# Two bursts of value products per head, half-ready one-hots and earlier first keys in a sparse-attention and soft-mixture block

## What is computed

```python
scores = jnp.einsum('bhqd,bhkd->bhqk', q, k) * scale
sparsity = scores.max(axis=-1) - scores.mean(axis=-1)
_, top_idx = jax.lax.top_k(sparsity, U)                 # U = 307
q_sel = jnp.take_along_axis(q, top_idx[..., None], axis=2)
scores_sel = jnp.einsum('bhud,bhkd->bhuk', q_sel, k) * scale
attn = jax.nn.softmax(scores_sel, axis=-1)
out_sel = jnp.einsum('bhuk,bhkd->bhud', attn, v)
out = jnp.zeros_like(q).at[bi, hi, top_idx].set(out_sel)
```

## Time and profile before

| what | us |
|---|---|
| median of 3 runs | 1648.62 (1648.59 to 1650.77) |
| the profiled execution, its own time | 1640.96 |
| its span in the trace | 1638.9 |
| attention of batch 0, first gather to last turn | 455.3 to about 596 |
| attention of batch 1 | 952.8 to about 1091 |

### The profile page before, as it was taken

One profiled execution on the slowest core, in us unless ns is written; L12 is line 12 of the kernel. 1 busy time (PEld: TensorE's weight loads), 2 busy tenths in 40 slices (PEclk: granted clock), 3 DMA queues, 4 the chain that ended last, 5 costly groups with the idle time before them and its releaser, 6 DMA issues.

```text
span 1638.9 us, 28513 instructions
## 1 busy us (share of the span) xinstructions
PE 1501.4 (92%) x8674; PEld 837.0 (51%) x8674; DVE 1218.9 (74%) x2910; ACT 1041.9 (64%) x1404; POOL 267.0 (16%) x317
## 2 busy tenths in 40 slices
PE   7989999998779999999998989989999999989999
PEld 3532222223345532222222745544788986479988
DVE  6689999999866759999999887856756443675511
ACT  4588888887546678888887547763343473333464
POOL 2430000004413362000000213341111000111100
PEclk9999999999989999999999999999999999999999
DMA  5751111131522201111112211120134302014410
GB/s 187 245 154 39 51 45 39 39 97 39 165 63 68 64 19 39 50 47 39 39 40 89 67 32 50 53 64 24 39 123 162 102 29 77 0 33 156 163 48 32
DMA packets 93457, 119.38 MB, mean 73 GB/s; under 512 B 22862, under 2 KB 78766, under 8 KB 92860
## 3 DMA queue, kind: packets, MB, share of 16 engines
q1 hardware_dynamic: 90300, 117.66, 23.5%
q0 software_dynamic: 3072, 0.66, 0.4%
HBM read 93.46 MB, written 24.79 MB: 72 GB/s over the span
## 4 chain that ended last, share of the span: by engine, by line
PE 46%; DVE 33%; issue 13%; DMA 3%; ACT 3%; POOL 1%; SPq 0%; DVEq 0%; ACTq 0%; POOLq 0%
DVE work_area L1239 25%; PE psum L2045 7%; PE psum L2109 6%; PE psum L1890 5%; PE psum L1913 5%; PE psum L1988 4%; PE psum L1904 4%; PE psum L2056 3%; DVE big_area L1239 2%; PE psum L2065 2%; DMA work_area<-heads_out 2%; PE psum L2099 2%; PE psum L1746 1%; PE psum L1721 1%; ACT big_area L919 1%
## 5 line engine op out<-in xcount | busy, mean ns | idle before, releaser
L1239 DVE CUSTOM_DVE_ANT_0 work_area<-psum,work_area 128x1024 f32<-128x1024 f32 x512 | 589.3, 1220 | 9.5 <-PE psum L1782 5.5
L849 ACT ACTIVATE work_area<-psum 128x1024 f32<-128x1024 f32 x512 | 510.4, 1026 | 78.1 <-DVE big_area L1239 29.1
L1782 PE MATMUL psum<-work_area 96*128 96x512 bf16 x1024 | 310.7, 385 | 48.1 <-DVE big_area L1239 7.5
L1772 PE MATMUL psum<-work_area 96*128 96x512 bf16 x1024 | 306.0, 381 | 7.7 <-ACT work_area L849 2.3
L1782 PEld LDWEIGHTS psum<-work_area 96*128 96x128 bf16 x1024 | 63.8, 97 | 266.9 <-DVE big_area L1239 250.8
L867 ACT ACTIVATE work_area<-psum 128x614 f32<-128x614 f32 x192 | 124.0, 681 | 87.7 <-PE psum L1904 87.5
L1772 PEld LDWEIGHTS psum<-work_area 96*128 96x128 bf16 x1024 | 89.1, 98 | 153.3 <-ACT work_area L849 58.6
L703 POOL DMA_INDIRECT heads_out<-work_area x96 | 98.0, 1021 | 190.9 <-DVE work_area L1394 169.8
L1988 PE MATMUL psum<-slots_T,work_area 128*128 128x512 f32 x256 | 117.5, 603 | 0.0
L2045 PE MATMUL psum<-work_area,xn 128*128 128x128 f32 x1024 | 117.2, 275 | 0.0
L2109 PE MATMUL psum<-expert_out,work_area 128*128 128x256 f32 x512 | 115.6, 379 | 1.1 <-ACT work_area L984 1.1
(11 more groups left out here) (255 smaller groups left out, 2046.4 us busy)
## 6 DMA issues: line engine op xcount, KB each, us to landing
work_area<-in_L_ffn_w_dram SPq DMA_DIRECT2D x32, 1024.0 KB, 5.5
work_area<-k_parts SPq DMA_DIRECT2D x192, 64.2 KB, 2.1
work_area<-q_parts SPq DMA_DIRECT2D x192, 64.0 KB, 2.2
k_parts<-work_area SPq DMA_DIRECT2D x24, 384.0 KB, 4.0
q_parts<-work_area SPq DMA_DIRECT2D x16, 384.0 KB, 2.5
big_area<-q_parts SPq DMA_DIRECT2D x16, 384.0 KB, 5.3
work_area<-k_parts SPq DMA_DIRECT2D x32, 192.0 KB
x_res<-in_L_attn_x_dram SPq DMA_DIRECT2D x8, 512.0 KB, 6.7
```

The costliest lines, as they stand in the source:

```text
L849: s.activation(SC[:, t % 4], PS[:, 2 * (n % 2):2 * (n % 2) + 2].rearrange("p a n -> p (a n)"), ACT.Relu).then_inc(relu_done, 1)
L1239: v.tensor_tensor_reduce(SC[:, t % 4], PS[:, 4 + 2 * (t % 2):6 + 2 * (t % 2)].rearrange("p a n -> p (a n)"), SC[:, t % 4], 1.0, -3.0e38, A ...
L1772: last = mm(PS[:, 2 * (n % 2) + k], QS1[par][0:TERMS, t * P:(t + 1) * P], KS[par][0:TERMS, k * 512:(k + 1) * 512], start=True, stop=True)
L1782: last = mm(PS[:, 4 + 2 * (t % 2) + k], QS1[par][0:TERMS, t * P:(t + 1) * P], KS[par][0:TERMS, K1 + k * 512:K1 + (k + 1) * 512], start=Tru ...
```

## The change

Four things are changed, all in the attention or just ahead of it.

1. The value products of a head come in two bursts of eight key tiles in place of four bursts of four, and there are eight `PX` buffers in place of four. The new buffers overlap the parts' area, so in the first head of batch 0 ACT waits for the last parts (`parts_ready`) before the seventh exponential, and SP issues the next batch's terms only when the head's gather is done (`gathered`, h + 3).
2. The one-hot gives a signal at its half (`oh_half_ready`), and the gathers are cut into halves of eight: the second half for the next head stands after this head's steps 2 and 3, the first half for the head after next behind steps 6 and 7, ahead of `turn` and of the signal `k2_used`.
3. `take_queries` moves from ahead of the eighth exponential to behind the fourth (in the first head behind the sixth); `rows` moves from the third burst to ahead of steps 4 and 5.
4. SP fetches the first two heads' keys of batch 0 and the ones ahead of all stores of batch 1's parts; before, the ones stood behind the store of unit 8 and the keys behind that of unit 12. (The ones are the constant rows under the keys.)

```diff
@@ memory
+        PX_last = [a.take([2, UP]) for _ in range(2)]
...
+        a = Area(zeros, 2 * UP)
+        PX += [a.take([2, UP]) for _ in range(2)] + PX_last
@@ SP, attention_keys, and the order of the queue
                         if h < 14:
+                            sp.wait_ge(gathered, h + 3)
                             key_term(1, (h - 2) // 6 * DH, (h - 2) // 6, k)
...
+            key_ones(0)
+            for par in range(2):
+                first_keys(0, par)
             for u in range(NU):
                 parts_to_dram(1, u)
                 if u == share(G + 1)[-1]:
                     queries_to_sbuf(0, 3)
-                if u == 8:
-                    key_ones(0)
-                if u == 12:
-                    for par in range(2):
-                        first_keys(0, par)
@@ ACT
-                        act.wait_ge(p_used, b * 64 + i * 8 + (par * 4 + k // 2 + 1))
-                        slot = k % 4
-                        s.activation(PX[slot][:, :, 0:U], PS[:, 2 * (k % 2):2 * (k % 2) + 2, 0:U], ACT.Exp, scale=SCALE).then_inc(p_ready, 1)
+                        act.wait_ge(p_used, b * 32 + i * 4 + par * 2 + k // 4 + 1)
+                        s.activation(PX[k][:, :, 0:U], PS[:, 2 * (k % 2):2 * (k % 2) + 2, 0:U], ACT.Exp, scale=SCALE).then_inc(p_ready, 1)
...
-                    for k in range(7):
+                    first = i == 0 and par == 0
+                    for k in range(8):
+                        if b == 0 and first and k == 6:
+                            act.wait_ge(parts_ready, B * NU)
                         exps(i, par, (k,))
-                        if b == 0 and i == 0 and par == 0 and 1 <= k <= 3:
+                        if b == 0 and first and 1 <= k <= 3:
                             second_part(1, NU - 4 + k)
-                    if more:
-                        take_queries(i, 1 - par, par + 1)
-                    exps(i, par, range(7, 8))
++                        if more and k == (5 if first else 3):
+                            take_queries(i, 1 - par, par + 1)
@@ DVE, onehot
+                        if not pieces and t == NT // 2 - 1:
+                            last.then_inc(oh_half_ready, 1)
@@ PE
-                            pe.wait_ge(oh_ready, b * H + i * 2 + (n + 1))
+                            pe.wait_ge(oh_half_ready, b * (H - 1) + i * 2 + n)
...
+                        elif t == NT // 2:
+                            pe.wait_ge(oh_ready, b * H + i * 2 + (n + 1))
...
-                def pe_head(i, n, first, later):
-                    CUTS = (0, 0, NT // 2, NT) if first else (0, 5, 11, NT)
-                    for k4 in range(3):
-                        scores(i, n, 2 * k4 + 2)
-                        scores(i, n, 2 * k4 + 3)
-                        values(i, n, k4)
-                        if k4 < 2 and later > 0:
-                            gather(i, n + 1, range(CUTS[k4 + 1], CUTS[k4 + 2]))
-                        if k4 == 2:
-                            if first and b == 1:
-                                pe.wait_ge(x1_done, NT + 2)
-                            rows(i, n)
-                            if not first:
-                                turn(i, n - 1)
+                def pe_head(i, n, later):
+                    first, second = i == 0 and n == 0, i == 0 and n == 1
+                    for k in (2, 3):
+                        scores(i, n, k)
+                    if later > 0 and not first:
+                        gather(i, n + 1, range(0 if second else NT // 2, NT))
+                    if first and b == 1:
+                        pe.wait_ge(x1_done, NT + 2)
+                    rows(i, n)
+                    for k in (4, 5):
+                        scores(i, n, k)
+                    values(i, n, 0)
+                    if first:
+                        gather(i, n + 1, range(NT))
+                    for k in (6, 7):
+                        scores(i, n, k)
+                    if later > 1 and not first:
+                        gather(i, n + 2, range(NT // 2))
+                    if not first:
+                        turn(i, n - 1)
                     pe.wait_ge(s_ready, b * 128 + i * 16 + (n * 8 + 8))
                     pe.sem_inc(k2_used, 1)
                     for k in range(2):
                         if later > 0:
                             scores(i, n + 1, k)
-                    values(i, n, 3)
-                    if later > 1:
-                        gather(i, n + 2, range(0, 5))
+                    values(i, n, 1)
```

More of the change, by code:

```diff
@@ L1905, in scores, with values @@
                     last.then_inc(s_ready, 1)
-                def values(i, n, k4):
-                    if k4 == 0:
+                def values(i, n, half):
+                    if half == 0:
                         pe.wait_ge(oT_used, max(0, b * H + i * 2 + n - 1))
-                    pe.wait_ge(p_ready, b * 128 + i * 16 + (n * 8 + 2 * k4 + 4))
-                    for q in range(4):
-                        kt = 4 * k4 + q
-                        last = mm(PS[32 * q:32 * q + DH + 1, 6 - n % 2, 0:U], V[:, kt, i * 2 + n], PX[kt // 2 % 4][:, kt % 2, 0:U], start=(kt < 4), stop=(kt >= NT - 4), skip_group_check=True)
+                    pe.wait_ge(p_ready, b * 128 + i * 16 + (n * 8 + 4 * half + 6))
+                    for kt in range(half * (NT // 2), (half + 1) * (NT // 2)):
+                        at = 32 * (kt % 4)
+                        last = mm(PS[at:at + DH + 1, 6 - n % 2, 0:U], V[:, kt, i * 2 + n], PX[kt // 2][:, kt % 2, 0:U], start=(kt < 4), stop=(kt >= NT - 4), skip_group_check=True)
                     last.then_inc(p_used, 1)
```

7 lines of the change are left out of this document (4 added, 3 removed).

## The result

The changed kernel takes 1644.07 us (median of 8 runs, 1641.21 to 1648.16), the kernel before beside it 1650.55 (8 runs, 1647.06 to 1654.69). The ratio is 0.9961, interval 0.9947 to 0.9974: 6.4 us faster, between 4.3 and 8.7. I had forecast 11.2. The traces hide this gain: the profiled execution of the changed kernel took 1642.25 us, that of the kernel before 1640.96, which none of its timed runs reached. That difference is most of the story.

The account below looks back on a forecast made before the run. PE bounded the kernel, with waits for the fetch in batch 0; after the change the fetch would bound both batches. 2.3 + 2.8 + 3.0 + 3.1 = 11.2 us, 1648.6 - 11.2 = 1637.4; forecast 1632 to 1641, range 1625 to 1649.

Parts of the forecast that it names:

- first heads of batch 1: Start of batch 1's attention: the new order and half signal were to save 3 us, bounds 0 and 5.
- batch 0, heads 3 to 13: Eleven heads of batch 0: from 8.35 to 8.1 us a head, 2.8 us in all.
- first heads of batch 0: Start of batch 0's attention: head 0 a little longer, later heads give that back, gain 0.
- batch 1, heads 3 to 13: Eleven heads of batch 1: from 7.98 to 7.7 us a head, 3.1 us in all.
- The bursts on PE: Value products: two bursts of eight take 2.64 us against 3.12, saving 0.48 a head; PE needs 7.43.
- The fetch is the bound: SP's key fetch, not PE, bounds heads in both batches: 8.1 us in batch 0, 7.7 in batch 1.
- The edits that cost nothing: Half one-hot signal, ACT's buffer wait and SP's terms wait: no wait worth a sum, the half signal's up to 0.2 us.
- First keys: Ahead of PE's first gather: ACT's 4.66 us wait for a store goes, gain 2.3 us, bounds 0 and 4.66.
- The base: Gain of 11.2 us taken from the median 1648.6, 7.7 us above the profiled execution's 1640.96.
- PE the bound: Rival for the heads: the fetch shrinks too, heads take 7.43 us, total 1627.2 us; chance 0.16.
- nothing in the heads: Rival: only the start and first heads gain, 2 to 5 us, total 1645 us; chance 0.15.
- held release: Rival: a wait at the half one-hot holds the release; at 0.5 us some 5 us, 1642; chance 0.09.

Follow-up runs that it names:

- e9: The kernel before with POOL's three scatters of a head replaced by plain transfers, their placing left out: 1641.17 us, 0.9905 of the kernel before.
- e17: The kernel of e9 again, in five rounds on the same chip as e18: 1640.10 us, 0.9938 of the kernel before.
- e8: The changed kernel with POOL's three scatters of a head replaced by plain transfers, their placing left out: 0.9901 of the kernel before.
- e16: The kernel of e8 again (changed kernel, plain transfers in place of scatters): 1631.73 us, 0.989 of the kernel before.
- e18: The kernel of e16 again (changed kernel, plain transfers), in five rounds on the same chip as e17: 1631.16 us, 0.9892 of the kernel before.
- e12: The kernel before, unchanged, once more with its trace: 1654.2 us, one execution.
- e5: The changed kernel with each fetch of keys as six transfers of 16 rows instead of three of 48, 32 and 16: 0.999 of the kernel before.
- e7: The changed kernel without the fetches of keys from the third head of each batch on: 0.9901 of the kernel before.
- e3: The changed kernel without SP's wait for the gather ahead of the two 64 KB terms of batch 0's heads: 0.9954 of the kernel before.
- e2: The changed kernel with `rows` behind the half gather, directly ahead of `turn`, instead of ahead of scores 4: 0.9914 of the kernel before.
- e6: The kernel before with each fetch of keys as six transfers of 16 rows: 0.9991 of the kernel before.
- e4: The kernel before with only the ones and first keys of batch 0 sent ahead of the stores of batch 1's parts: 0.9983 of the kernel before.
- e10: The kernel of e2 with POOL's scatters of a head begun only behind the second burst of the next head: 0.9923 of the kernel before.
- e11: The changed kernel with the same wait on POOL as e10 and nothing else: 0.9944 of the kernel before.
- e1: The changed kernel with ACT's copy of the queries behind exponential 4 instead of 3, in every head but the first: 0.9993 of the kernel before.
- e13: The changed kernel with POOL's second scatter of a head waiting for scores 4 and the third for scores 7: 1.0454 of the kernel before.
- e14: The kernel of e2 with the scatters spaced as in e13: 1.0254 of the kernel before.
- e15: The kernel before with the scatters spaced as in e13: 1.0220 of the kernel before.

## Why the prediction was right and wrong

The sign held; the size didn't. The measured 1644.07 lies outside the 1632 to 1641 that was given a chance of 0.50, though inside the outer 1625 to 1649. Two steps of the prediction failed. One is that the fetch bounds a head and that the runs differ from the trace by a mere offset of 7.7 us: in the usual execution a head waits for PE's late signals and takes 8.69 and 7.97 us, not 8.1 and 7.7. The other is the term of 3.0 us for the first heads of batch 1, which was read from one execution at a lower clock than others have there; at the same clock the traces give 1.2.

Heads and stages, by the first exponential of a head, as means of two traces of before (e9, e17) and three of the changed kernel (e8, e16, e18) without scatters, beside what the prediction said, and traces with held signals (e12, changed):

| step | forecast gain | without holds | with holds (e12, changed) |
|---|---|---|---|
| first keys, to the first gather | 2.3 | 12.9 to 11.05: 1.9 | 12.6 to 11.05: 1.5 |
| batch 0, heads 3 to 13 | 2.8 (8.35 to 8.1 a head) | 8.27 to 7.95 a head: 3.5 | 9.15 to 8.69: 5.1 |
| first heads of batch 0 | 0 | 28.6 to 28.5: 0.1 | 31.0 to 28.4: 2.6 |
| first heads of batch 1 | 3.0 | 29.3 to 29.2: 0.1 | 27.8 to 28.2: -0.4 |
| batch 1, heads 3 to 13 | 3.1 (7.98 to 7.7) | 8.08 to 7.80: 3.1 | 8.44 to 7.97: 5.2 |

The right column sets one execution against one. Timed runs of the kernel before lie between 1646.0 and 1659.5 us over all chips, so they carry more or fewer holds, and its 14 us are no estimate for the medians.

- **The bursts on PE: right.** 1.16 us and not the 1.5 that would have been wrong. A head of PE's work in e18's chain is four groups of scores at 0.63, two bursts at 1.16, two half gathers at 1.06, turn 0.33 and rows 0.15, 7.44 us, against 7.43 forecast. That the totals agree is in part luck: the groups of scores cost 0.63, not the 0.53 of the earlier trace rows, 0.4 us more in a head, and turn and rows together 0.48, not 0.73.
- **The fetch is the bound: right where no signal is held, wrong in the usual execution.** e18 shows the forecast's picture, the 0.44 us of idleness included. With held signals a faster fetch (e5) or none (e7) doesn't bring heads back to it: 9.10 and 8.55 in batch 0.
- **The edits that cost nothing.** The half signal costs nothing: the gathers of eight stand in the chain right behind the scores. The terms' wait costs nothing (e3). What was missing from that list is `rows`. I had put its 0.25 us into the sum as mere PE time; ahead of scores 4 it moves their signal further into the hold, and taking it away from there brings 8 us (e2). The two traces show 3.8 of them in heads 3 to 13 of batch 0 and 0.4 in those of batch 1.
- **First keys: right in size**, 1.9 for 2.3, and wrong in one link: I let the store go early once SP is free of the keys. In e6 it leaves 2.1 us later than before and the wait is gone all the same, so the cost lay in the store's own 12.0 us behind the keys' long transfers.
- **The first heads of batch 1: wrong, 3.0 us for 1.2.** The term rested on one execution, in which these heads took 30.8 us (987.7 - 956.9, by their exponentials); the same order took 27.8 in e6, e9 and e12 and 30.9 in e17. The order isn't what changes between them, and neither is the wait at 979.39 for ACT's table: e12 has it too, with the same 1.59 us, and the changed kernel with 1.36 at 981.95. It is the granted clock. Rows of the first trace (windows, columns as in the earlier trace rows), then of e12, windows and PE's timeline:

```profile
964.00:967.00 3.00, 1.92 (x19) 0.57 (x15) 3.00 (x16) 2.14 (x5) 0.00 (x0) 1.00 0.13 22
967.30:970.70 3.40, 3.12 (x17) 1.62 (x17) 3.40 (x20) 1.05 (x2) 0.00 (x0) 0.50 0.18 60
980.90:984.30 3.40, 3.40 (x22) 1.85 (x18) 1.15 (x5) 1.22 (x3) 0.38 (x1) 0.51 0.10 30
...
979.00:984.00 5.00, 5.00 (x49) 2.68 (x46) 3.99 (x22) 3.01 (x5) 0.00 (x0) 1.00 0.09 36
988.65 1.01 PE L1904 MATMUL psum<-work_area 99*128 99x307 bf16 x4 [1.59 <-ACT work_area L867]
```

In the first trace the clock stood at half, the lower of its two levels (1.2 and 2.4 GHz), for two stretches of 3.4 us, the first one behind a stretch in which PE was busy for 1.92 of 3 us; in e12 it stayed at 1.00. Sorted by the number of such stretches the lengths fall in place: in the order of before 27.8 us with none (e6, e9, e12) and 30.8 to 30.9 with two (the first trace, e4, e17); in the order of after 27.8 to 28.3 with one (changed, e2, e3, e5, e10, e16) and 29.6 to 29.9 with two (e7, e8, e11, e18, and e1, where they follow each other). So with two stretches in both the order brings 1.2 us, and the 0.1 of the table is a mean over executions with unlike clocks. The prediction had the clock among its bounds, but not in the row that it read. Without the 3 us the sum is 8.2, with 1.2 in their place 9.4, and e17 against e18 measures 7.6 to 8.9.

- **The base: wrong.** I added the sum to a median 7.7 us above the trace I had read, and treated those 7.7 us as an offset with no place in the kernel. Most of them were held signals: before's own median falls 9 us (1648.9 to 1640.1, e17) and 14 (1655.4 to 1641.2, e9) with the scatters replaced. The bound that I found was that of a rare execution. The changed kernel loses to them as well, 0.9961 against 0.9892, 11 us. So both kernels carry holds of about the same cost, 9 to 14 us and 11; that the changed one pays 1 or 2 us more would take 7.6 to 8.9 down to the 6.4 measured, but the intervals are too wide to show it.

Of the rivals, "PE the bound" and "nothing in the heads" didn't come. The "held release" came in another form: not at the half one-hot, but through PE's own late signals.

## What to carry to other kernels

Before costing an edit, compare the profiled execution with the timed ones. If it is quicker than all of them, its critical chain is not the one that is timed, and a second trace is worth more than a finer sum. A stage of some 30 us that is read from one trace should be read with its clock: here two stretches of 3.4 us at half made 3 us. Scores or any producer whose signal another engine needs at once shouldn't fall on POOL's second and third back-to-back scatter; a quarter of a microsecond of other work put ahead of it can decide that. And before an engine off the critical path is given a wait, find out who reuses its buffers.

## What the hardware showed that I had not expected

While POOL issued indirect transfers back to back, signals of PE came up to 2.1 us later than usual (scores 4 in e5: 2.39 us after their last matmul's start in place of 0.31; bursts in e10: 2.35 in place of 0.47), though its array worked on; several were then raised 0.04 us apart (scores 4 and 5 in e4: 512.93 and 512.97). With plain transfers from the same queue there was none in five traces. In these traces scatters are needed for it but not enough, since the first trace of before has them and no hold. What makes the difference between two executions of one kernel is open.

One more number goes with it: how many raised semaphores the trace recorded.

| traces | records |
|---|---|
| without a held signal: before, e8, e9, e16, e17, e18 | 17,413 to 17,448 |
| held: changed, e1 to e4, e10 to e12 | 16,121 to 16,348 |
| spaced: e13, e14, e15 | 16,904, 16,887, 17,143 |

In executions with held signals about 1,100 records are missing, most of them landings of transfers (10,708 in the changed kernel's trace, 11,711 in the first of before). The runs e5 to e7 have other numbers of transfers and can't be set beside these. The Trainium skill, "NOTIFIC — the notification-queue block", "Overflow: three behaviours, one of which stalls the engine", says that the block which writes such records holds back its producers when its inner queues are full, by which it could throttle an engine, rather than lose a record there. Late signals would agree with the first half and the missing records don't agree with the second, unless they are lost elsewhere; no run here tells whether recording makes the holds or suffers from them.
